# QKV of a transformer block on one core: normalized tokens turned by VectorE and moved within SBUF instead of turned by TensorE

## The chip, the core and the metric

The kernel runs on one core of a Trainium2 chip. TensorE (PE in the profile) multiplies, VectorE (DVE) and ScalarE (ACT) work on elements, GpSimd (POOL) does little here, and SyncE (SP) issues nearly every transfer. The metric is the device time of one execution in microseconds (us).

## The reference

One block of a diffusion transformer on 4096 tokens of 576 channels (2 batches of 2048), in float32, with 16 heads of 36 channels. Six vectors per batch come from a condition and shift, scale and gate the two halves.

```python
ada = silu(c) @ W_ada + b_ada
shift_msa, scale_msa, gate_msa, shift_mlp, scale_mlp, gate_mlp = split(ada, 6)
h = layernorm(x) * (1 + scale_msa) + shift_msa
x = x + gate_msa * attention(h, W_qkv, b_qkv, W_proj, b_proj)
h = layernorm(x) * (1 + scale_mlp) + shift_mlp
x = x + gate_mlp * (gelu(h @ W_fc1 + b_fc1) @ W_fc2 + b_fc2)
```

The change touches only the making of `h` for the first product, `h @ W_qkv`.

## The kernel before

The kernel has four phases: QKV (`phase_qkv`, the first 405 us of the span), attention, projection, MLP. Each engine has its own function (`sync`, `tensor`, `vector`, `scalar`, `gpsimd`), its instructions run in the order in which that function writes them, and semaphores join them.

QKV goes over the tokens in 8 chunks `c` of 512. A chunk has 13 steps `k`: four V steps (`k` 0 to 3, two products of 128 tokens by 288 channels each) and nine QK steps (`k` 4 to 12, called QK0 to QK8 here; one product of 128 channels by 512 tokens). Each product is 14 matmuls, since float32 accuracy is made of a high part (`hh`) and a rest (`lo`) of the tokens and of the weights. The product needs the tokens turned: channels on partitions. For that, the next chunk is prepared in ten pieces `n`, spread over the steps of the current one by the function `step(c, k)`, which all engines share:

- `n` 0 and 1: VectorE takes mean and variance of the token rows in `xin` (L823, L827), ScalarE the root (L953), VectorE the reciprocal;
- `n` 2 and 3: VectorE writes the normalized tokens into `xn` (L834), with 64 of the channels a second time, since the last of the five channel groups has only 64 and is held twice;
- `n` 5 to 9, one per channel group `kt`: TensorE turns four blocks of 128 by 128 into PSUM (`pt`, L667), ScalarE scales and shifts them into `hf` (L966), VectorE casts to `hh` (L846) and subtracts for `lo` (L849, L852).

`hf` has two buffers. From the second chunk on, `step` puts piece `n` at step `k = n`, so the last piece comes at `k` 9, which is QK5. A product of a chunk (L720) waits until all five `lo` of its own chunk are there (`s_lo`).

A QK result goes from PSUM (four buffers `pm`, shared with V) through ScalarE twice: `tf` (L1000) and its rounding `th` (L1001). VectorE subtracts for `tl` (L927), and SyncE stores `th` and `tl` to HBM (L628, L630). `tf`, `th` and `tl` have two buffers each, so ScalarE's L1000 of QKn waits until the stores of the QK two before have landed (`s_qo`). At QK2, SyncE loads `xin` for the chunk after next (L535), at V3 it stores V (L638). In the first chunks a row of the modulation (`modulation`, L682 on TensorE) lies in some QK steps; the step numbers are those of `mod_step`: one such product each in the chunks 0, 1, 2 and 3.

Of the kernel before, what the change touches and what calls it, by code (L numbers as in the profile page):

```python
# [7 lines left out]
F = mybir.dt.float32  # L8
# [7 lines left out]
C = 576  # L16
# [390 lines left out]
def phase_qkv(nc, A, ident, adaT, eps, bq, sc, qs0, ks0, qb0, hh0, lo0, mx, gd, xf, cond, W_ada,  # L407
# [46 lines left out]
    s_cond, s_ident, s_cz = A.sem("cond"), A.sem("ident"), A.sem("cz")  # L454
    s_ct, s_sc, s_am0, s_row0 = A.sem("ct"), A.sem("sc"), A.sem("am0"), A.sem("row0")
    s_vhi, s_vlo, s_qhi, s_qlo = A.sem("vhi"), A.sem("vlo"), A.sem("qhi"), A.sem("qlo")
    s_q0, s_q1, s_s, s_mx = A.sem("q0"), A.sem("q1"), A.sem("s"), A.sem("mx")
    s_nm, s_mt, s_mh, s_m = A.sem("nm"), A.sem("mt"), A.sem("mh"), A.sem("m")
    s_bv, s_bn, s_st, s_sd, s_rs, s_xn = (A.sem("bv"), A.sem("bn"), A.sem("st"), A.sem("sd"), A.sem("rs"),
                                          A.sem("xn"))  # L460
    s_tp, s_hf, s_hh, s_lo = A.sem("tp"), A.sem("hf"), A.sem("hh"), A.sem("lo")
    s_mm, s_tf, s_tl, s_vc, s_on = A.sem("mm"), A.sem("tf"), A.sem("tl"), A.sem("vc"), A.sem("on")
    s_qo, s_vo = A.sems("qo", 2), A.sems("vo", 2)

# [63 lines left out]

    def sync(e):
        def load(c):
            if c > 1:
                e.wait_ge(s_xn, c - 1)
            e.dma_start(xin[c % 2][:, :, :], xf[c * CH:(c + 1) * CH, :].rearrange("(t p) c -> p t c", p=128)).then_inc(  # L535
                s_x[c % 2], 16)
# [61 lines left out]
        def second_loads():  # L598
            e.wait_ge(s_mm, UN * (NCH - 1))
            e.wait_ge(s_q0, 128)  # L600
            for dst, r, src, f0, n, t, w in rows_b(qb0, ks0[:, LK:L], qkh, qkl, 0, C, 0):
                e.dma_start(dst[r:r + n, :].bitcast(F), src[f0:f0 + n, t:t + w]).then_inc(s_q1, 16)

        def max_rows():
            for j, m in enumerate((mh, ml)):
# [5 lines left out]
        for c in range(NCH):  # L611
            if c == HCH:
                first_loads()
            elif c == NCH - 1:
                second_loads()
            for kind, n in steps(c):
                if kind == "qk":
                    vi, p = mod_step(c, n)
                    if vi is not None:
                        modulation(vi, p)  # L620
                    if (c, n) == (NCH - 1, 7):
                        max_rows()
                    ft, j = c * NF + n, n % 2
                    if last(c, kind, n):
                        continue
                    rows, cols = slice(n * 128, n * 128 + 128), slice(c * CH, (c + 1) * CH)
                    e.wait_ge(s_tf, ft + 1)
                    e.dma_start(qkh[rows, cols], th[j][:, :].bitcast(F)).then_inc(s_qo[j], 16)  # L628
                    e.wait_ge(s_tl, ft + 1)
                    e.dma_start(qkl[rows, cols], tl[j][:, :].bitcast(F)).then_inc(s_qo[j], 16)  # L630
                    if n == 2 and c + 2 < NCH:
                        load(c + 2)
                elif n == 3:
                    b, k = divmod(c, HCH)
                    e.wait_ge(s_vc, 8 * (c + 1))
                    if c < 2:
                        e.wait_ge(s_on, c + 1)
                    e.dma_start(vd[b * H:(b + 1) * H, :, k * 4 * VW:(k + 1) * 4 * VW].rearrange("h p n -> p h n"),  # L638
                                vx[c % 2][:, :, :, :].rearrange("p h t d -> p h (t d)")).then_inc(s_vo[c % 2], 16)
        e.wait_ge(s_qo[0], 32 * (NCH * 5 - 1))  # L640
        e.wait_ge(s_qo[1], 32 * NCH * 4)
        for i in range(2):
            e.wait_ge(s_x[i], 16 * HCH)
            e.wait_ge(s_vo[i], 16 * HCH)
        for i in range(KT):
            e.wait_ge(s_wv[i], 16 if i < 4 else 32)
# [3 lines left out]
        e.wait_ge(s_wa, 128)  # L650
        e.wait_ge(s_bad, 128)
        e.wait_ge(s_gd, 32)
        e.wait_ge(s_q0, 128)
        e.wait_ge(s_q1, 128)
        e.wait_ge(s_m, 64)

    def tensor(e):
# [129 lines left out]
        for c in range(NCH):  # L787
            h, l = hh[c % 2], lo[c % 2]
            for k, (kind, n) in enumerate(steps(c)):
                if kind == "qk":  # L790
                    vi, p = mod_step(c, n)
                    if vi is not None:
                        modulation(vi, p)
                for m in maxima(c, kind, n):
                    score_max(m)
                if (c, kind, n) == (NCH - 1, "qk", 5):
                    max_rows()
                if (c, kind, n) == (0, "v", 0):
                    first_products()
                elif (c, kind, n) == (0, "v", 1):  # L800
                    pass
                elif kind == "qk":
                    product(c, 8 + n, passes(wh, wl, wm, wr, h, l, slice(n * 128, n * 128 + 128), slice(0, CH)),
                            pm[(c * UN + 8 + n) % 4][:, :])
                else:
                    for n2 in range(2):
                        u = 2 * n + n2
                        product(c, u, passes_t(wh, wl, wm, wr, h, l, slice(2 * C + n2 * HALF, 2 * C + (n2 + 1) * HALF),
                                               slice(n * 128, n * 128 + 128)), pm[(c * UN + u) % 4][:, 0:HALF])
                if c + 1 < NCH:  # L810
                    for p in step(c, k):
                        prepare(c + 1, p)

    def vector(e):
        def prepare(c, n):
            i = c % 2
            if n < 2:
                e.wait_ge(s_x[i], 16 * (c // 2 + 1))
                if c:
                    e.wait_ge(s_tp, KT * c)  # L820
                for t in range(2 * n, 2 * n + 2):
                    for g in range(2):
                        e.bn_stats(st[:, t, g, :], xin[i][:, t, g * HALF:(g + 1) * HALF]).then_inc(s_bn, 1)  # L823
            if n == 1:
                for t in range(4):
                    e.wait_ge(s_bn, 8 * c + 2 * t + 2)
                    e.bn_aggr(mv[:, t, :], st[:, t, :, :]).then_inc(s_st, 1)  # L827
                e.wait_ge(s_sd, c + 1)
                e.reciprocal(rs[:, :], sd[:, :]).then_inc(s_rs, 1)
            elif n in (2, 3):  # L830
                e.wait_ge(s_rs, c + 1)
                for t in range(2 * n - 4, 2 * n - 2):
                    for a, z, d in ((0, C, 0), (512, C, C)):
                        ins = e.tensor_scalar(xn[:, t, d:d + z - a], xin[i][:, t, a:z], mv[:, t, 0:1], rs[:, t:t + 1],  # L834
                                              ALU.subtract, ALU.mult)
# [112 lines left out]
    def scalar(e):  # L948
        def prepare(c, n):
            if n == 1:  # L950
                e.wait_ge(s_st, 4 * (c + 1))
                e.wait_ge(s_cz, 2)
                e.activation(sd[:, :], mv[:, :, 1], ACT.Sqrt, bias=eps[:, 0:1]).then_inc(s_sd, 1)  # L953
            elif 5 <= n < 10:
                kt, b = n - 5, c // HCH
                k = c * KT + kt
                j = k % 2
                e.wait_ge(s_tp, k + 1)
                if k > 1:
                    e.wait_ge(s_lo, k - 1)  # L960
                if k == 0:
                    e.wait_ge(s_row0, 9)
                if k < 3:
                    e.activation(hh[0][:, kt, :], pt[j][:, :], ACT.Identity, bias=adaT[:, 0, kt, b:b + 1],
                                 scale=adaT[:, 1, kt, b:b + 1]).then_inc(s_hh, 1)
                e.activation(hf[j][:, :], pt[j][:, :], ACT.Identity, bias=adaT[:, 0, kt, b:b + 1],  # L966
                             scale=adaT[:, 1, kt, b:b + 1]).then_inc(s_hf, 1)

        e.wait_ge(s_ct, 1)
# [1289 lines left out]
```

## Time and profile before

| | us |
|---|---|
| median of 3 runs (3258.19 to 3258.70) | 3258.28 |
| the profiled execution | 3255.73 |
| its span | 3254.0 |
| PE busy | 3238.2 (100%) |
| DVE busy | 2161.4 (66%) |
| ACT busy | 1695.6 (52%) |
| POOL busy | 358.3 (11%) |
| transfers on SyncE's queue, packets | 187582 (34.1% of 16 engines' span) |

The granted TensorE clock is 0.999 of full speed as a mean over the span. A busy TensorE says only that a matmul was in flight: matmuls overlap, so the pace is read from the distance of their starts, and a wait from the gap between an end and the next start.

### The profile page before, as it was taken

How to read it: one execution, taken by the hardware profiler on the slowest of the kernel's cores; microseconds unless marked ns; L12 is line 12 of the kernel's file. 1: busy time of each engine (PE TensorE's matmuls, PEld its weight loads, DVE VectorE, ACT ScalarE, POOL GpSimd, SP SyncE). 2: the span in 40 equal slices, each digit the busy share in tenths (PEclk: the TensorE clock that was granted, in tenths of full speed). 3: DMA queues.
4: the chain of work that ended last, by engine and by line, in shares of the span. 5: the costliest groups of instructions: out<-in, count | busy, mean ns of one | idle time of the engine just before them, and what ended most of it. 6: DMA issues, size and time to landing. Idle time of an engine off the chain costs nothing. (4 is left out here: it accounts for less than half of the span.)

```text
span 3254.0 us, 52481 instructions
## 1 busy us (share of the span) xinstructions
PE 3238.2 (100%) x19049; PEld 2117.3 (65%) x19049; DVE 2161.4 (66%) x4134; ACT 1695.6 (52%) x3183; POOL 358.3 (11%) x284
## 2 busy tenths in 40 slices
PE   9999999999999999999999999999999999999999
PEld 7888744444444444444444444449998898989988
DVE  6444488888888888888888888857633433433332
ACT  4323377777777777777777777765611112211110
POOL 0000010111100000010000000026411010000000
PEclk9999999999999999999999999999999999999999
DMA  7554442333323232323232333328722122421211
GB/s 241 179 165 149 153 93 59 75 74 76 66 59 66 59 65 56 68 63 69 59 69 59 65 63 65 63 63 276 238 95 77 53 82 71 142 69 57 80 46 55
DMA packets 187841, 299.53 MB, mean 92 GB/s; under 512 B 66783, under 2 KB 87791, under 8 KB 180670
## 3 DMA queue, kind: packets, MB, share of 16 engines
q1 hardware_dynamic: 187582, 296.17, 34.1%
q8 instruction: 151, 2.47, 0.3%
q14 instruction: 108, 0.88, 0.1%
HBM read 193.99 MB, written 101.43 MB: 91 GB/s over the span
## 5 line engine op out<-in xcount | busy, mean ns | idle before, releaser
L1306 DVE TENSOR_REDUCE q_mx<-b_st 128x1 f32<-128x512 f32 x1512 | 988.6, 681 | 147.8 <-PE b_st L1240 142.8
L1380 ACT ACTIVATE b_pt<-b_st 128x512 f32<-128x512 f32 x2048 | 1055.1, 609 | 8.6 <-PE b_st L1256 8.5
L1268 PE MATMUL b_op<-b_pt,b_vs 128*37 128x512 f32 x4096 | 981.5, 600 | 2.1 <-DVE b_ob L1349 2.1
L1373 ACT ACTIVATE b_early<-b_st 128x512 f32<-128x512 f32 x504 | 302.3, 600 | 451.3 <-PE b_st L1240 451.3
L1268 PEld LDWEIGHTS b_op<-b_pt,b_vs 128*37 128x37 f32 x4096 | 203.5, 113 | 444.3 <-issue 360.2
L2125 PE MATMUL d_pm<-d_vh,d_ah 128*128 128x288 f32 x1152 | 339.3, 295 | 0.8 <-DVE d_al L2163 0.8
L2126 PE MATMUL d_pm<-d_vl,d_ah 128*128 128x288 f32 x1152 | 339.5, 295 | 0.0
L2127 PE MATMUL d_pm<-d_vh,d_al 128*128 128x288 f32 x1152 | 339.5, 295 | 0.0
L1306 DVE TENSOR_REDUCE q_mx<-b_early 128x1 f32<-128x512 f32 x504 | 339.4, 673 | 0.0
L1444 POOL TENSOR_TENSOR w_oc<-b_oa,b_ob 37x512 f32<-37x512 f32 x127 | 161.3, 1270 | 1440.4 <-DVE b_ob L1349 1437.4
L1240 PEld LDWEIGHTS b_st<-q_hh,b_qa 36*128 36x128 f32 x1024 | 128.7, 184 | 223.5 <-DVE q_mx L1306 197.7
L1240 PEld LDWEIGHTS b_st<-q_ks,q_qs 36*128 36x128 f32 x992 | 125.1, 184 | 221.8 <-DVE q_mx L1306 193.6
L1240 PE MATMUL b_st<-q_hh,b_qa 36*128 36x512 f32 x1024 | 231.1, 444 | 0.0
L1240 PE MATMUL b_st<-q_ks,q_qs 36*128 36x512 f32 x992 | 225.8, 447 | 3.1 <-PEq L1025 2.0
L2174 DVE TENSOR_TENSOR d_ug<-d_pm,d_gt 128x288 f32<-128x288 f32 x128 | 58.5, 457 | 245.8 <-PE d_pm L2127 245.8
L2125 PEld LDWEIGHTS d_pm<-d_vh,d_ah 128*128 128x128 f32 x1152 | 216.2, 188 | 1.7 <-issue 1.0
L2126 PEld LDWEIGHTS d_pm<-d_vl,d_ah 128*128 128x128 f32 x1152 | 216.1, 188 | 0.7
L2127 PEld LDWEIGHTS d_pm<-d_vh,d_al 128*128 128x128 f32 x1152 | 216.2, 188 | 0.0
L1256 PE MATMUL b_st<-q_lo,q_ks 46*128 46x512 f32 x1024 | 205.6, 395 | 0.0
L1253 PE MATMUL b_st<-b_qa,q_hh 64*128 64x512 f32 x1024 | 205.5, 396 | 0.0
L1253 PE MATMUL b_st<-q_qs,q_ks 64*128 64x512 f32 x1024 | 205.3, 396 | 0.0
L1256 PE MATMUL b_st<-b_qb,q_hh 46*128 46x512 f32 x1024 | 204.9, 394 | 0.0
(414 smaller groups left out, 4685.7 us busy)
## 6 DMA issues: line engine op xcount, KB each, us to landing
qkh<-a_th SPq DMA_DIRECT2D x72, 256.0 KB, 2.1
qkl<-a_tl SPq DMA_DIRECT2D x72, 256.0 KB, 2.3
d_yi<-y SPq DMA_DIRECT2D x64, 288.0 KB, 3.0
n_oi<-hw SPq DMA_DIRECT2D x12, 1024.0 KB, 5.8
vd<-a_vx SPq DMA_DIRECT2D x8, 1184.0 KB, 6.6
b_vs<-vd SPq DMA_DIRECT2D x32, 296.0 KB, 3.0
a_x<-in_x SPq DMA_DIRECT2D x8, 1152.0 KB, 6.8
q_qs<-qkh SPq DMA_DIRECT2D x32, 288.0 KB
```

The lines of the kernel that those rows point to most:

```text
L1240: e.matmul(bank(slots[a])[:, :], qa[i][r, queries], ka[i][r, keys], start=True, stop=True).then_inc(s_s, 1)
L1253: e.matmul(bank(slots[a])[:, :], ka[i][r, keys], qa[i][r, queries], start=True, stop=False)
L1256: e.matmul(bank(slots[a])[:, :], kb[i][r, keys], qb[i][r, queries], start=False, stop=True).then_inc(s_st, 1)
L1268: ins = e.matmul(op[64 * a:64 * a + VW, :], vs[h % 2][:, j + 8 * a, :], pt[g % NP][:, a * 512:a * 512 + 512], start=j == 0, stop=j == 7)
L1306: e.tensor_reduce(mx[:, k // 2, col:col + 1], src, AX.X, ALU.max).then_inc(s_mx, 1)
L1373: e.activation(early[:, :], bank(slot)[:, :], ACT.Copy).then_inc(s_cp, 1)
L1380: e.activation(pt[g % NP][:, a * 512:a * 512 + 512], bank(k)[:, :], ACT.Exp, scale=SCALE).then_inc(s_p, 1)
L1444: e.tensor_tensor(oc[i][:, :], oa[i][:, :], ob[i][:, :], ALU.add).then_inc(s_oc, 1)
L2125: e.matmul(out, ah[:, f, ts], vh[:, f, cs], start=f == 0, stop=False)
L2126: e.matmul(out, ah[:, f, ts], vl[:, f, cs], start=False, stop=False)
L2127: ins = e.matmul(out, al[:, f, ts], vh[:, f, cs], start=False, stop=f == NT - 1)
L2174: e.tensor_tensor(ug[m % 2][:, :], pm[m % 4][:, 0:HALF], gt[:, b, cs], ALU.mult).then_inc(s_ug, 1)
```

## The change

Chunk 0 is prepared as before. For chunks 1 to 7, TensorE's four transposes per channel group are gone. Instead:

- a chunk of `xin` is loaded by four transfers of 32 partitions each, so that the tokens stand in the order that blocks of 32 by 32 need;
- VectorE no longer writes the 64 channels a second time; a new piece `n` 4 turns 32 by 32 blocks from `xn` back into `xin`, four instructions of 128 by 576;
- SyncE moves the turned blocks from `xin` into `xn`'s memory (`turned`) by 24 transfers of 32 partitions with runs of 512 bytes (`move`), written ahead of QK1's stores (QK3's in chunk 0);
- ScalarE reads `turned` in SBUF and waits for all 24 (`s_xl`);
- `step` has new places: pieces 5 to 9 come at `k` 9, 10, 10, 11, 12 (chunk 0: 10, 10, 11, 11, 12).

```diff
     def step(c, k):
         if c:
-            return range(k, k + 1)
-        return range(2) if k == 3 else range(k - 2, k - 1) if k in (4, 5) or 7 <= k < 12 else range(0)
+            return {9: range(5, 6), 10: range(6, 8), 11: range(8, 9), 12: range(9, 10)}.get(k, range(k, min(k + 1, 5)))
+        return {3: range(2), 4: range(2, 3), 5: range(3, 4), 6: range(4, 5), 10: range(5, 7), 11: range(7, 9),
+                12: range(9, 10)}.get(k, range(0))
...
+            for i in range(4):
+                rows = slice(c * CH + i * 128, c * CH + i * 128 + 128)
+                e.dma_start(xin[c % 2][i * 32:i * 32 + 32, :, :], xf[rows, :].rearrange("(t p) c -> p t c", p=32)).then_inc(
+                    s_x[c % 2], 16)
+
+        def move(c):
+
+            e.wait_ge(s_tp, KT + c)
+            blocks = xin[c % 2][:, :, :].rearrange("p t c -> p (t c)").rearrange("p (j r) -> p j r", r=128)
+            for i in range(4):
+                src, tok = blocks[i * 32:i * 32 + 32], slice(i * 128, i * 128 + 128)
+                for j in range(4):
+                    p, n = slice(j * 32, j * 32 + 32), 5 if j < 2 else 4
+                    e.dma_start(turned[p, 0:n, tok], src[:, j:4 * n - 3 + j:4, :]).then_inc(s_xl, 16)
+                    if j > 1:
+                        e.dma_start(turned[p, 4, tok], src[:, 14 + j, :]).then_inc(s_xl, 16)
...
                 if kind == "qk":
+                    if c + 1 < NCH and n == (1 if c else 3):
+                        move(c + 1)
...
-                if c + 1 < NCH:
-                    for p in step(c, k):
-                        prepare(c + 1, p)
...
+            elif n == 4 and c:
+                e.wait_ge(s_xn, c + 1)
+                blocks = xin[i][:, :, :].rearrange("p t c -> p (t c)").rearrange("p (j t c) -> p j t c", t=4, c=32)
+                for t in range(4):
+                    ins = e.transpose(blocks[:, :, t, :], xn[:, t, 0:C].rearrange("p (j c) -> p j c", c=32))
+                ins.then_inc(s_tp, 1)
...
-                e.wait_ge(s_tp, k + 1)
+                if c:
+                    e.wait_ge(s_xl, 16 * MOVES * c)
+                else:
+                    e.wait_ge(s_tp, k + 1)
...
-                e.activation(hf[j][:, :], pt[j][:, :], ACT.Identity, bias=adaT[:, 0, kt, b:b + 1],
+                e.activation(hf[j][:, :], turned[:, kt, :] if c else pt[j][:, :], ACT.Identity, bias=adaT[:, 0, kt, b:b + 1],
```

ScalarE at the end of chunk 1, from QK5 on, before (L1000 and L1001 write `tf` and `th`, L966 writes `hf`):

```order
L966 ACTIVATE a_hf<-a_pt,g_adaT 128x512 [waits a_s_lo,a_s_tp]
L1000 ACTIVATE a_tf<-a_pm,g_bq 128x512 [waits a_s_qo1,a_s_mm]
L1001 ACTIVATE a_th<-a_pm,g_bq 128x512
L966 ACTIVATE a_hf<-a_pt,g_adaT 128x512 [waits a_s_lo,a_s_tp]
L1000 ACTIVATE a_tf<-a_pm,g_bq 128x512 [waits a_s_qo0,a_s_mm]
L1001 ACTIVATE a_th<-a_pm,g_bq 128x512
L1000 ACTIVATE a_tf<-a_pm,g_bq 128x512 [waits a_s_qo1,a_s_mm]
L1001 ACTIVATE a_th<-a_pm,g_bq 128x512
L1000 ACTIVATE a_tf<-a_pm,g_bq 128x512 [waits a_s_qo0,a_s_mm]
L1001 ACTIVATE a_th<-a_pm,g_bq 128x512
```

And the same stretch of the changed kernel (L1032, L1033 and L998 are the same three lines):

```order
L998 ACTIVATE a_hf<-a_xn,g_adaT 128x512 [waits a_s_lo,a_s_xl]
L1032 ACTIVATE a_tf<-a_pm,g_bq 128x512 [waits a_s_qo0,a_s_mm]
L1033 ACTIVATE a_th<-a_pm,g_bq 128x512
L998 ACTIVATE a_hf<-a_xn,g_adaT 128x512 [waits a_s_lo,a_s_xl] x2
L1032 ACTIVATE a_tf<-a_pm,g_bq 128x512 [waits a_s_qo1,a_s_mm]
L1033 ACTIVATE a_th<-a_pm,g_bq 128x512
L998 ACTIVATE a_hf<-a_xn,g_adaT 128x512 [waits a_s_lo,a_s_xl]
L1032 ACTIVATE a_tf<-a_pm,g_bq 128x512 [waits a_s_qo0,a_s_mm]
L1033 ACTIVATE a_th<-a_pm,g_bq 128x512
L998 ACTIVATE a_hf<-a_xn,g_adaT 128x512 [waits a_s_lo,a_s_xl]
```

The last piece stood ahead of QK6's evacuation; now it stands behind QK8's, the last of the chunk.

SyncE in chunk 1, from QK0's second store to QK1's, in the changed kernel (L557 and L559 are the moves; before, QK1's store followed QK0's directly):

```order
L655 DMA qkl<-a_tl 128x512 [waits a_s_tl]
L557 DMA a_xn<-a_x 32x5x128 [waits a_s_tp]
L557 DMA a_xn<-a_x 32x5x128
L557 DMA a_xn<-a_x 32x4x128
L559 DMA a_xn<-a_x 32x128
L557 DMA a_xn<-a_x 32x4x128
L559 DMA a_xn<-a_x 32x128
```

These six stand there four times, and then QK1's stores, a modulation row, QK2's stores and the load of `xin` in four parts:

```order
L653 DMA qkh<-a_th 128x512 [waits a_s_tf]
L655 DMA qkl<-a_tl 128x512 [waits a_s_tl]
L585 DMA gd<-a_row 2x576 [waits a_s_row]
L653 DMA qkh<-a_th 128x512 [waits a_s_tf]
L655 DMA qkl<-a_tl 128x512 [waits a_s_tl]
L546 DMA a_x<-in_x 32x4x576 [waits a_s_xl]
L546 DMA a_x<-in_x 32x4x576 x3
```

On VectorE, the turning stands between QK0's `tl` and QK1's. TensorE's first V product of the next chunk, the consumer of all of it, still waits for the last `lo` and for a PSUM buffer:

```order
L744 MATMUL a_pm<-a_hh,a_wr 128x512
L744 MATMUL a_pm<-a_wh,q_hh 128x288 [waits a_s_tf,a_s_lo]
L744 MATMUL a_pm<-a_wl,q_hh 128x288
L744 MATMUL a_pm<-a_wh,q_lo 128x288
L744 MATMUL a_pm<-a_wh,q_hh 128x288
```

## Rows read from the trace of the kernel before

**Rows 1.** Waits from 60 to 350 us: who waited for whom, total, times, longest.

```profile
ACT a_tf L1000 <- PE a_pm L720: 128.9, 48, 8.1
...
ACT a_tf L1000 <- DMA qkl<-a_tl: 16.2, 5, 4.7
```

**Rows 2.** Stretches: us, busy PE, PEld, DVE, ACT, POOL, granted clock, DMA share, GB/s.

```profile
240.00:270.00 30.00, 30.00 (x164) 26.02 (x163) 13.51 (x25) 12.02 (x19) 0.00 (x0) 1.00 0.50 180
```

**Rows 3.** Timeline of TensorE in chunk 3: start, length, instruction.

```profile
204.28 0.60 PE L667 MATMUL a_pt<-g_ident,a_xn 128*128 128x128 f32 x4
...
207.92 0.39 PE L720 MATMUL a_pm<-a_hh,a_wh 128*128 128x512 f32 x1
...
210.87 0.39 PE L720 MATMUL a_pm<-a_hh,a_wr 128*128 128x512 f32 x1
211.19 2.69 PE L682 MATMUL a_sp<-a_wa,g_sc 128*2 128x288 f32 x20
```

**Rows 4.** Groups of instructions, first 600 us: count, busy us, mean ns, idle before.

```profile
L667 PE MATMUL a_pt<-g_ident,a_xn 128*128 128x128 f32 x160 | 23.8, 272 | 0.0
...
L834 DVE TENSOR_SCALAR a_xn<-a_x,a_mv,a_rs 128x576 f32<-128x576 f32 x64 | 24.1, 440 | 0.0
...
L1319 DVE STREAM_TRANSPOSE b_nt<-b_nm 128x32 f32<-128x32 f32 x14 | 3.0, 211 | 0.5
```

**Rows 5.** Timeline of TensorE: the last matmul of chunk 3.

```profile
216.89 0.39 PE L720 MATMUL a_pm<-a_hh,a_wr 128*128 128x512 f32 x1
```

**Rows 6.** Timeline of ScalarE in chunk 3.

```profile
190.43 0.78 ACT L966 ACTIVATE a_hf<-a_pt,g_adaT 128x512 f32<-128x512 f32 x1
...
196.53 0.68 ACT L1001 ACTIVATE a_th<-a_pm,g_bq 128x512 fp32r<-128x512 f32 x1
197.10 0.78 ACT L966 ACTIVATE a_hf<-a_pt,g_adaT 128x512 f32<-128x512 f32 x1
197.77 0.69 ACT L1000 ACTIVATE a_tf<-a_pm,g_bq 128x512 f32<-128x512 f32 x1
...
206.60 0.69 ACT L1000 ACTIVATE a_tf<-a_pm,g_bq 128x512 f32<-128x512 f32 x1 [3.84 <-DMA qkl<-a_tl]
...
217.32 0.69 ACT L1000 ACTIVATE a_tf<-a_pm,g_bq 128x512 f32<-128x512 f32 x1 [4.29 <-PE a_pm L720]
217.90 0.68 ACT L1001 ACTIVATE a_th<-a_pm,g_bq 128x512 fp32r<-128x512 f32 x1
```

**Rows 7.** Timeline of VectorE in chunk 3.

```profile
191.24 0.43 DVE L846 CAST q_hh<-a_hf 128x512 fp32r<-128x512 f32 x1
191.70 0.69 DVE L849 TENSOR_TENSOR q_lo<-a_hf,q_hh 128x512 fp32r<-128x512 f32 x1
...
218.62 0.69 DVE L927 TENSOR_TENSOR a_tl<-a_tf,a_th 128x512 fp32r<-128x512 f32 x1 [3.55 <-ACT a_th L1001]
```

**Rows 8.** Timeline of SyncE's issues: start, time of issuing, transfer.

```profile
25.23 1.11 SPq L481 DMA_DIRECT2D a_xn<-in_L_cond_W_qkv  x2
...
198.33 0.45 SPq L535 DMA_DIRECT2D a_x<-in_x  x1
...
199.79 0.32 SPq L630 DMA_DIRECT2D qkl<-a_tl  x1
...
221.79 0.37 SPq L596 DMA_DIRECT2D q_ks<-qkh  x1
...
224.26 0.39 SPq L596 DMA_DIRECT2D q_ks<-qkh  x1
```

**Rows 9.** Transfers from 60 to 350 us: count, KB each, median us from issue to landing.

```profile
qkl<-a_tl SPq DMA_DIRECT2D x55, 256.0 KB, 2.4
vd<-a_vx SPq DMA_DIRECT2D x6, 1184.0 KB, 6.4
```

**Rows 10.** Timeline of TensorE: first matmul behind the gap between QKV and attention.

```profile
407.44 0.50 PE L1240 MATMUL b_st<-q_ks,q_qs 36*128 36x512 f32 x2 [2.04 <-PEq L1025]
```

**Rows 11.** The stretch behind that gap, columns as in the second group.

```profile
409.00:414.50 5.50, 5.25 (x18) 2.96 (x19) 5.33 (x9) 4.73 (x10) 4.14 (x6) 0.50 0.95 264
```

More of the change, by code:

```diff
@@ L456, in phase_qkv @@
     s_vhi, s_vlo, s_qhi, s_qlo = A.sem("vhi"), A.sem("vlo"), A.sem("qhi"), A.sem("qlo")
-    s_q0, s_q1, s_s, s_mx = A.sem("q0"), A.sem("q1"), A.sem("s"), A.sem("mx")
+    s_q0, s_s, s_mx = A.sem("q0"), A.sem("s"), A.sem("mx")
     s_nm, s_mt, s_mh, s_m = A.sem("nm"), A.sem("mt"), A.sem("mh"), A.sem("m")
@@ L463, in phase_qkv @@
     s_qo, s_vo = A.sems("qo", 2), A.sems("vo", 2)
+    s_xl = A.sem("xl")
+    MOVES = 24
     vx0, vx1 = [q[:, :, :, :].rearrange("p h t d -> p (h t d)") for q in vx]
@@ L472, in phase_qkv @@
     sq = wa0[2:5] + [xf0[:, 0:2 * C], xf0[:, 2 * C:4 * C]]
+    turned = xf0.rearrange("p (k r) -> p k r", r=CH)
     V, QK = slice(2 * C, 3 * C), slice(0, 2 * C)
@@ L532, in load @@
         def load(c):
[L533 to L536, printed above, removed]
+            if c == 0:
+                e.dma_start(xin[0][:, :, :], xf[0:CH, :].rearrange("(t p) c -> p t c", p=128)).then_inc(s_x[0], 16)
+                return
+            if c == 2:
+                e.wait_ge(s_xn, 1)
+            elif c > 2:
+                e.wait_ge(s_xl, 16 * MOVES * (c - 2))
+            for i in range(4):
[12 more added lines that the diff above has]
+                        e.dma_start(turned[p, 4, tok], src[:, 14 + j, :]).then_inc(s_xl, 16)
         def columns(vi):
@@ L601, in second_loads @@
             for dst, r, src, f0, n, t, w in rows_b(qb0, ks0[:, LK:L], qkh, qkl, 0, C, 0):
-                e.dma_start(dst[r:r + n, :].bitcast(F), src[f0:f0 + n, t:t + w]).then_inc(s_q1, 16)
+                e.dma_start(dst[r:r + n, :].bitcast(F), src[f0:f0 + n, t:t + w]).then_inc(s_q0, 16)
         def max_rows():
@@ L642, in sync @@
         for i in range(2):
-            e.wait_ge(s_x[i], 16 * HCH)
+            e.wait_ge(s_x[i], 64 * HCH - 48 * (1 - i))
             e.wait_ge(s_vo[i], 16 * HCH)
@@ L652, in sync @@
         e.wait_ge(s_gd, 32)
-        e.wait_ge(s_q0, 128)
-        e.wait_ge(s_q1, 128)
+        e.wait_ge(s_q0, 256)
         e.wait_ge(s_m, 64)
@@ L817, in prepare @@
             if n < 2:
-                e.wait_ge(s_x[i], 16 * (c // 2 + 1))
-                if c:
-                    e.wait_ge(s_tp, KT * c)
+                e.wait_ge(s_x[i], 64 * (c // 2 + 1) - 48 * (1 - i))
+                if c == 1:
+                    e.wait_ge(s_tp, KT)
+                elif c:
+                    e.wait_ge(s_hf, KT * c)
                 for t in range(2 * n, 2 * n + 2):
@@ L832, in prepare @@
                 for t in range(2 * n - 4, 2 * n - 2):
-                    for a, z, d in ((0, C, 0), (512, C, C)):
+                    for a, z, d in ((0, C, 0),) if c else ((0, C, 0), (512, C, C)):
                         ins = e.tensor_scalar(xn[:, t, d:d + z - a], xin[i][:, t, a:z], mv[:, t, 0:1], rs[:, t:t + 1],
```

## The prediction, made before the changed kernel had run

> **What bounds the kernel now.** I read the stretches first: in QKV, TensorE is busy 30.00 of 30 us at full clock [rows 2]. Then the waits: from 60 to 350 us none is TensorE's; ScalarE waits 128.9 us for TensorE, and 16.2 us for the store that frees its buffers [rows 1]. So QKV runs at TensorE's pace. What TensorE no longer does is gained in full, and a wait of TensorE is lost in full, unless it is caught up, and an engine that is the bound has nothing to catch up with. The timelines then give the pace of each engine and the handovers, from which the new waits have to be worked out.
>
> **What is removed.** With one group of four transposes in it, a QK step takes from 204.28 to 207.92, 3.64 us. Without, 14 matmuls at a distance of (210.87 - 207.92)/13 = 0.227 us take 3.18 us [rows 3]. So a group of four costs 0.46 us, although the mean of one instruction is 272 ns [rows 4]: they overlap. There are 160 in all, 20 of them chunk 0's; 140 go, 35 groups by 0.46 = **-16.1 us**. The wait of transposes on `hf` goes too; it cost nothing. VectorE's 28 short second writes go, worth nothing either, since VectorE is busy 13.5 of 30 us [rows 2].
>
> **What the new order adds at each chunk's end.** Before, the last `hf` of the next chunk was made in step QK5, three steps (9.5 us) ahead of its use, and V followed QK8 without a gap: no wait of TensorE stands there [rows 1, 2]. Now ScalarE makes it behind QK8's evacuation, and the first V product waits for the `lo` made of it. Even with every engine ready, from the start of QK8's last matmul (216.89 in chunk 3 [rows 5]):
>
> - ScalarE begins `tf` at 217.32: 0.43; `th` 0.58 later [rows 6];
> - `hf` 0.57 after `th` (196.53 to 197.10), and it takes 0.78 [rows 6];
> - VectorE's `tl` begins at 218.62, 0.72 after `th`, and takes 0.69 [rows 7], which ends just when `hf` does; the cast begins 0.03 after `hf`'s end (190.43 + 0.78 = 191.21, then 191.24), the subtraction 0.46 after the cast, and takes 0.69 [rows 6, 7];
> - some 0.05 to TensorE, as in the other handovers.
>
> Sum 0.43 + 0.58 + 0.57 + 0.78 + 0.03 + 0.46 + 0.69 + 0.05 = 3.59, less the 0.23 at which the next matmul would have followed anyway [rows 3]: 3.36 us of wait. Nothing covers it: all PE work of the chunk is done, and the next chunk's needs this `lo`. Seven boundaries: +23.5 us, already more than the 16.1 saved. Piece by piece this is the surest term; its rows exist, only `hf`'s source is now SBUF.
>
> **What the moves add.** SyncE issues in order. The nearest rows of few partitions are the eight loads of 28 to 36 partitions: from 221.79 to 224.26 six distances, 0.41 us each [rows 8]. Bounds: 0.36 (a store's 0.32 [rows 8] and a gap of 0.04) and 0.56 (64 partitions, 1.11 for two [rows 8]) plus 0.04. I take 0.41, by 24 = 9.8 us (8.6 to 14.4). The data are 7 x 2560 packets of 512 bytes; a store of V, 2048 packets (16 by 128 rows of 592 bytes), lands in 6.4 us [rows 9], so the 2560 of a chunk need about 8.0 us with their latency, less than the issuing. VectorE's four turns of 128x576 have no row: a turn of 128x32 takes 211 ns, a pass over 576 columns 440 ns [rows 4], and a pass of 512 at 0.69 gives 0.78 for 576 [rows 7]. From 0.4 to 0.78; I take 0.70, 2.8 us, since the turn of 32 columns has no sign of the faster pass.
>
> The Trainium skill ("Vector Engine (DVE) Microarchitecture Reference", 3.8 The reshape front-end) says that the transpose sustains one element per cycle per lane. By that and the 0.96 GHz of "VectorE: DVE Perf Modes", 576 columns are an estimated 0.60 us, so 2.4 us for four; no row shows it, and the sum would be the same within 0.5 us a chunk.
>
> Now one chunk without a modulation product but with a load of `xin` (chunks 4, 5), in us from QK0's first matmul; QKn ends at 3.18(n+1) + 0.2:
>
> - `tf` of QK0 at 3.4, its `tl` done at 5.4, the turns at 8.2, the last move issued at 18.0;
> - QK1's stores stand behind the moves: `tl` issued at 18.4, landed 2.4 later [rows 9], 20.8. ScalarE can't begin QK3's `tf` before, where it began at 12.9. TensorE would need that buffer for QK7 at 22.3; `th` is ready at 22.1. So no stall there, by a hair;
> - QK2's stores, and the load of `xin` in four issues by 0.46, till 21.0. QK3's `tl` store is issued at 22.8 behind this load. In the row of such a store it was issued at 199.79, 1.46 after the load, and ScalarE went on at 206.60 [rows 6, 8], 8.2 after the load's issue. From the middle of the four issues that gives 28.2; I take 28 for QK5's `tf`;
> - from there ScalarE is the bound: `tf` and `th` 1.17 a pair, `hf` 0.67 each [rows 6]. QK6 29.8, two `hf`, QK7 32.4, one, QK8 34.2, and the last `hf` 35.4 to 36.1; 1.25 to the `lo` and TensorE: 37.4. V could have begun at 28.6: **8.8 us** of wait.
>
> Chunk 6 has no load: QK5's `tf` at 25.2, V at 34.6, 6.0. Chunks 1 to 3 have a modulation product of 2.6 to 2.7 us [rows 3] on TensorE, which puts off its own need: 8.8 - 2.7 = 6.1 each. Chunk 0 moves two steps later, with load ahead of moves, and has a modulation product too: tf of QK5 at 27.1, last `lo` at 37.2, need at 31.3: 5.9. Sum 2 x 8.8 + 6.0 + 3 x 6.1 + 5.9 = **+47.8 us**, the 23.5 of the order being part of it.
>
> **The clock.** A gap of 2.04 us at the end of QKV [rows 10] was followed by 5.5 us at a granted clock of 0.50, which is 1.2 in place of 2.4 GHz [rows 11]: 5.25 us busy at half pace, 2.6 lost. The seven new gaps are each longer. I take 2.6 for each, **+18.2 us**; bounds 0 (if the clock rides over such a gap) and, since each stretch may be longer than this one, 3.5.
>
> **The sum**: -16.1 + 47.8 + 18.2 = +49.9 on the profiled execution's 3255.7, 3305.6. The median of runs is 2.5 above that execution, which I keep: **3308 us**.
>
> **Rivals.**
> 1. The moves hide, only the order costs. If the stores behind them get through in time (shorter issues, a load that passes aside), each gap is 3.36: +23.5 - 16.1 = +7.4, 3266 without any drop of the clock, 3284 with it. For it: TensorE needs QK3's buffer only at 22.3, and ScalarE waits for TensorE 128.9 us in all [rows 1], which is room to catch up. Against it: 24 by even 0.36 still puts the last issue at 16.8. The Trainium skill ("DMA: Bandwidth & Descriptors", Issuing engines are not separate DMA queues) speaks for it: the time on the sequencer to start transfers is "usually small relative to the DMA itself". By that rule the moves would hold SyncE for little. The trace disagrees for transfers this small: 0.41 us of issue [rows 8] for one twenty-fourth of some 8 us, and nothing gained.
> 2. The moves are slower than issued: 0.60 us each, because the issues cost what those of 64 partitions do, or because all read from 32 partitions. The last move is then 4.6 us later, at 22.6, QK3's `tf` at 25.4, TensorE stands at QK7 for about 4.7, and all behind is later: about 4.6 x 7 = +32 more, 3340.
> 3. Faster: the gap at a boundary falls under 16.1/7 = 2.3 us, from where the removed transposes decide. For that the last `hf`, cast and subtraction would have to take 1.5 us in place of 2.5, with SBUF as source and no queue behind the moves. Full gain if the gap vanished, 3242; at a gap of 2.0, 3256. Against it: ScalarE's order alone holds `hf` back, and its rows vary by under 5%.
> 4. The change doesn't do what it says: should TensorE keep transposes or the moves be done earlier, no wait appears. The order shows the opposite.
>
> **How the numbers follow.** Forecast 0.62 (own range 3288 to 3330), rival 1 0.16, rival 2 0.16, rival 3 0.03, nothing to be told 0.03. Less than 0.2% (6.5 us) is no change that a measurement of this kernel tells. The range 3270 to 3344 leaves out rivals 3 and the lower part of 1 and upper part of 2. Faster 0.03, same 0.03, slower 0.94.
>
> **What would show it.** In the profile after: TensorE waits for VectorE's L881 seven times, 6 to 9 us each, over 40 us in sum, ahead of the first V product; granted clock 0.5 for some us behind each; L691 counts 20. ScalarE's waits for DMA `qkl` rise from 16 to 60 us or more. Move issues 0.41 us apart. QK steps end at 3.18 us. Wrong would be the forecast if gaps are 3.4 us (rival 1), if TensorE stands in the middle of a chunk (rival 2), or if no drop of the clock follows a gap of 6 us.

## The result and the profile after

| | before | after |
|---|---|---|
| median of 4 runs, us | 3258.24 (3257.81 to 3258.70) | 3363.82 (3361.08 to 3369.03) |
| profiled execution's span, us | 3254.0 | 3367.3 |
| TensorE's first matmul of attention, us | 407.44 | 515.24 |
| TensorE busy, us | 3238.2 | 3253.8 |

The changed kernel is slower: ratio 1.0324, 95% interval 1.0311 to 1.0337, 105.6 us where 50 were forecast. The direction was right, and the three costs of the forecast (order, moves, slower clock) are there; the size was not: 3363.8 lies above the range, and TensorE also stands in mid-chunk, where the forecast had no wait. The first matmul of attention moved by 107.8 us [rows 10], so nearly all of the loss is in QKV; the rest of the span differs by 5.5 us, and by 1 to 5.5 in the other versions.

The waits of the changed kernel from 20 to 520 us; before, TensorE had none in the middle of QKV and ScalarE waited 16.2 us for stores [rows 1]:

```profile
ACT a_tf L1032 <- DMA qkl<-a_tl: 150.1, 20, 18.1
...
PEld a_pm L744 <- DVE a_hh L881: 34.6, 4, 14.3
PE a_pm L744 <- DVE a_hh L881: 32.7, 3, 13.9
PE a_pm L744 <- ACT a_th L1033: 31.7, 6, 6.6
PEld a_pm L744 <- DVE q_hh L881: 28.2, 3, 11.1
PE a_pm L744 <- DVE q_hh L881: 26.9, 3, 10.6
...
PE a_sp L727 <- ACT a_hf L998: 3.1, 1, 3.1
```

The PE rows are the loss. TensorE waits at two places of a chunk: for the last `lo` of the next one (L881), 59.6 us at six boundaries and 3.1 at the seventh (behind a score product there), and in six of seven chunks for ScalarE's evacuation (L1033), 31.7 us. Sum 94.4. The PEld rows are the weight loads ahead of the same matmuls, not to be added. ScalarE's row says why: 150.1 us of waits for stores.

SyncE's issues in chunk 1, from QK0's second store on (start, time of issuing):

```profile
104.91 0.32 SPq L655 DMA_DIRECT2D qkl<-a_tl  x1
107.58 1.93 SPq L557 DMA_DIRECT2D a_xn<-a_x  x3
109.55 0.60 SPq L559 DMA_DIRECT2D a_xn<-a_x  x1
...
123.34 0.60 SPq L559 DMA_DIRECT2D a_xn<-a_x  x1
123.98 0.58 SPq L653 DMA_DIRECT2D qkh<-a_th  x1
124.61 0.43 SPq L655 DMA_DIRECT2D qkl<-a_tl  x1
...
126.36 2.05 SPq L546 DMA_DIRECT2D a_x<-in_x  x4
```

A move holds SyncE for 0.60 us, 0.65 from start to start, where 0.41 was read off [rows 8]. The block of 24 takes 16.4 us, from 107.58 to 123.98 (15.9 to 16.5 in the other chunks), and only then QK1's stores go. On ScalarE it looks so, in the same chunk; the bracket is its idle time before, and what ended it:

```profile
109.24 0.69 ACT L1032 ACTIVATE a_tf<-a_pm,g_bq 128x512 f32<-128x512 f32 x1 [1.91 <-PE a_pm L744]
...
127.06 0.69 ACT L1032 ACTIVATE a_tf<-a_pm,g_bq 128x512 f32<-128x512 f32 x1 [16.56 <-DMA qkl<-a_tl]
```

And on TensorE, at QK7 of chunk 1 and at the boundary behind it:

```profile
128.47 0.77 PE L744 MATMUL a_pm<-a_hh,a_wh 128*128 128x512 f32 x1 [3.73 <-ACT a_th L1033]
...
147.03 0.61 PE L744 MATMUL a_pm<-a_wh,q_hh 128*128 128x288 f32 x1 [10.63 <-DVE q_hh L881]
```

The clock behind that boundary (columns as in [rows 2]): 0.60 as a mean over six us, part of them at half clock, then full:

```profile
147.00:153.00 6.00, 5.97 (x29) 5.97 (x30) 0.46 (x1) 0.00 (x0) 0.00 (x0) 0.60 0.87 275
153.00:160.00 7.00, 7.00 (x55) 7.00 (x55) 5.06 (x17) 0.30 (x1) 0.00 (x0) 1.00 0.02 4
```

Of VectorE and TensorE in the changed kernel, by groups, as in [rows 4]:

```profile
L691 PE MATMUL a_pt<-g_ident,a_xn 128*128 128x128 f32 x20 | 2.9, 275 | 0.0
...
L865 DVE STREAM_TRANSPOSE a_x<-a_xn 128x576 f32<-128x576 f32 x28 | 19.2, 744 | 0.0
L857 DVE TENSOR_SCALAR a_xn<-a_x,a_mv,a_rs 128x576 f32<-128x576 f32 x32 | 17.2, 574 | 0.0
```

20 transposes are left, as forecast, and a turn takes 744 ns where 0.70 was taken.

To make an account, I took QKV in stretches of 1 us and summed TensorE's idle time, and its busy time by (1 - granted clock) as what the slower clock lost. For the changed kernel 94.4 idle and 28.4 of clock, from 34 us to the last matmul of QKV; with the 16.1 us saved, 94.4 + 28.4 - 16.1 = 106.7, against 107.8 measured at attention's first matmul. For the kernel before both are zero. The same account, over the same part, is given for each version below; for E1 (which saves nothing) to E9 it meets the shift of attention's first matmul within 1.1 us.

### The profile page after: what moved, and what is told of

Its sections match the earlier page's. It is cut to its first block and busy times, and to the rows that moved or that the text cites. A ratio compares the mean times of both kernels' runs of the same rounds, so it can differ in the third digit from the quotient of the medians.

```text
span 3367.3 us, 52354 instructions
## 1 busy us (share of the span) xinstructions
PE 3253.8 (97%) x18909; PEld 2131.1 (63%) x18909; DVE 2172.8 (65%) x4134; ACT 1694.6 (50%) x3183; POOL 358.7 (11%) x284
```

## The experiments

All are timed against the kernel before on the same chip. Its medians were 3256.9 (E1 to E4), 3258.5 (E5 to E8) and 3260.2 us (E9 to E11), so the ratios compare versions of different groups better than the medians. E5 is not in the table: it was executed once, for its issues (3338.6 us).

| version | median us | ratio (95%) | idle | clock |
|---|---|---|---|---|
| changed kernel | 3363.8 | 1.0324 (1.0311 to 1.0337) | 94.4 | 28.4 |
| E1 order only | 3286.4 | 1.0089 (1.0074 to 1.0104) | 20.9 | 8.3 |
| E2 no moves | 3277.9 | 1.0064 (1.0049 to 1.0079) | 22.0 | 12.4 |
| E3 24 small moves | 3361.3 | 1.0318 (1.0303 to 1.0334) | 91.2 | 26.5 |
| E4 4 wide moves | 3290.8 | 1.0101 (1.0085 to 1.0118) | 33.3 | 16.8 |
| E6 last piece earlier | 3358.3 | 1.0308 (1.0294 to 1.0322) | 86.7 | 29.5 |
| E7 moves spread | 3338.2 | 1.0245 (1.0231 to 1.0259) | 81.2 | 14.7 |
| E8 rebuilt, 16 moves | 3251.7 | 0.9978 (0.9968 to 0.9988) | 4.4 | 1.7 |
| E9 15 of 24 moves | 3324.6 | 1.0200 (1.0186 to 1.0214) | 62.3 | 18.2 |
| E10 rebuilt, even lots | 3248.4 | 0.9964 (0.9952 to 0.9977) | 1.3 | 0.0 |
| E11 rebuilt, half on GpSimd | 3250.7 | 0.9970 (0.9959 to 0.9981) | 3.3 | 0.0 |

**E1: the order alone.** The kernel before, with only `step` replaced:

```diff
 # before.py
-            return range(k, k + 1)
-        return range(2) if k == 3 else range(k - 2, k - 1) if k in (4, 5) or 7 <= k < 12 else range(0)
+            return {9: range(5, 6), 10: range(6, 8), 11: range(8, 9), 12: range(9, 10)}.get(k, range(k, min(k + 1, 5)))
+        return {3: range(2), 4: range(2, 3), 5: range(3, 4), 6: range(4, 5), 10: range(5, 7), 11: range(7, 9),
+                12: range(9, 10)}.get(k, range(0))
```

> The kernel before, with only the places of the pieces 5 to 9 of the change (last channel group at QK8); TensorE still turns. My theory: ScalarE makes the last hf behind QK8's evacuation, so TensorE waits at each of 7 boundaries 3.4 us less the 0.5 us that its own transposes take: +20 us, and up to 18 more if the clock falls behind each gap: 3278 to 3297. Rival A (the order costs nothing, all of the loss is the moves): 3258. Rival B (the order is most of the loss of 106 us): above 3320.

Measured 3286.4, 29.5 above before. TensorE's gap is 2.77 or 2.78 us at six boundaries, as here, and 1.68 ahead of a score product at the seventh:

```profile
73.26 0.40 PE L721 MATMUL a_pm<-a_wh,a_hh 128*128 128x288 f32 x1 [2.78 <-DVE a_hh L853]
...
221.26 0.63 PE L668 MATMUL a_pt<-g_ident,a_xn 128*128 128x128 f32 x4 [2.26 <-ACT a_hf L967]
```

2.78 us where 3.4 - 0.5 = 2.9 was expected; the second row is another wait, for a free `pt` ahead of the last transposes, in one chunk. The order costs by itself, and rival A falls; so does rival B, since this is far from the whole loss.

**E2: no moves.**

```diff
-                e.wait_ge(s_xl, 16 * MOVES * (c - 2))
+                e.wait_ge(s_tp, KT + c - 2)
...
         def move(c):
             e.wait_ge(s_tp, KT + c)
-            for i in range(4):
-                ...
-                    e.dma_start(turned[p, 0:n, tok], src[:, j:4 * n - 3 + j:4, :]).then_inc(s_xl, 16)
+            return
...
-                    e.wait_ge(s_xl, 16 * MOVES * c)
+                    e.wait_ge(s_tp, KT + c)
```

> The changed kernel without the 24 transfers of move() (what ScalarE reads is then not the turned tokens). VectorE's turns, the four loads and the places stay. My theory: 3258 - 16 + 23.5 = 3266, to 3284 if the clock falls behind each gap. Rival B (order and turns are most of the loss): above 3320.

Measured 3277.9, inside of what was expected; rival B falls. The gaps, the first two of seven:

```profile
70.94 0.40 PE L738 MATMUL a_pm<-a_wh,a_hh 128*128 128x288 f32 x1 [3.25 <-DVE a_hh L875]
120.71 0.61 PE L738 MATMUL a_pm<-a_wh,q_hh 128*128 128x288 f32 x1 [3.24 <-DVE q_hh L875]
```

3.24 us against 3.36 forecast: five of the six boundaries have 3.24 or 3.25, one 3.31, and the gap ahead of the score product at the seventh is 2.15. The clock differs behind gaps of the same length: behind the first it stayed at full, 1.00 from 70 to 78 us, and the next matmul took 0.40; behind the second it was 0.57 as a mean from 120 to 124 us, and the matmul took 0.61. This version has the turns, the four loads and the order, and costs 20.9 us; the changed kernel's other 84.7 us (105.6 less 20.9, each against its own before) are the moves.

**E3 and E4: issues or bytes.** E3 keeps 24 transfers but cuts each to one run; E4 keeps the bytes and packets but in 4 transfers of 128 partitions.

```diff
 # E3
-                    e.dma_start(turned[p, 0:n, tok], src[:, j:4 * n - 3 + j:4, :]).then_inc(s_xl, 16)
+                    e.dma_start(turned[p, 0, tok], src[:, j, :]).then_inc(s_xl, 16)
 # E4
+                e.dma_start(turned[:, 0:5, i * 128:i * 128 + 128], blocks[:, i:13 + i:3, :]).then_inc(s_xl, 16)
```

> The changed kernel with all 24 transfers a chunk, but each moves only one run of 512 bytes a partition (16 KB), 384 KB a chunk in place of 1310 KB. Theory of the issue (each transfer holds SyncE 0.65 us, whatever it carries): 3355 to 3364, as the changed kernel. Rival C (the bytes moved within SBUF hold up the stores behind them): nearer to the kernel without moves, under 3310.

> The changed kernel with the same 1310 KB and 2560 packets a chunk, but in 4 transfers of 128 partitions in place of 24 of 32 partitions (what lands is not the turned tokens). Theory of the issue: 20 issues by 0.65 = 13 us fewer ahead of QK1's stores, so near the kernel without moves: 3268 to 3292. Rival C (bytes): 3350 to 3364.

Measured 3361.3 and 3290.8. Over the version without moves, 24 issues with 29% of the bytes cost 83.4 us, 4 issues with all bytes 13.0, both together 84.7. So nearly all of the cost is in the number of issues; rival C falls as the main cause. SyncE in E3, and then in E4:

```profile
171.77 1.80 SPq L557 DMA_DIRECT2D a_xn<-a_x  x3
173.61 0.59 SPq L559 DMA_DIRECT2D a_xn<-a_x  x1
...
187.66 0.58 SPq L653 DMA_DIRECT2D qkh<-a_th  x1
```

```profile
152.14 3.16 SPq L554 DMA_DIRECT2D a_xn<-a_x  x4
155.35 1.09 SPq L648 DMA_DIRECT2D qkh<-a_th  x1
156.48 0.96 SPq L650 DMA_DIRECT2D qkl<-a_tl  x1
```

An issue of 16 KB holds SyncE for 0.59 us, one of 80 KB in the changed kernel for 0.61; the block is 15.9 us long, like there. In E4 a wide one (320 KB) takes 0.79 to 0.80 in five of the seven chunks, 1.2 to 1.3 in two, and the stores behind it 1.09 and 0.96, where they took 0.58 and 0.43 behind the changed kernel's moves: there the bytes do show.

**E5: what makes an issue dear.** 20 transfers a chunk, whose form changes by chunk:

```diff
+                n = (128, 64, 48, 36, 28, 32, 36)[c - 1]
+                src = blocks[0:n, i % 18, :] if c < 6 else xf[c * CH + i:c * CH + i + n, 0:128]
+                e.dma_start(turned[0:n, kt, tok], src).then_inc(s_xl, 16)
```

> A look at the issuing time alone: the changed kernel with 20 transfers a chunk of one run of 512 bytes a partition, whose number of partitions differs by chunk: 128, 64, 48, 36, 28 within SBUF, then 32 and 36 from HBM (what lands is not the turned tokens). Theory D (few partitions make an issue dear): the time rises from 0.36 us at 128 to 0.65 at 64 and below. Theory E (source and target both in SBUF make it dear): 0.65 for all five within SBUF, about 0.4 for the two from HBM. Theory F (the number divided over the 16 queues): 0.65 where the number is a multiple of 16 other than 128 (64, 48, 32), 0.4 at 36 and 28, which divide over 12 and 14.

The issues of its one execution (start, time of all 20):

```profile
53.03 13.18 SPq L557 DMA_DIRECT2D a_xn<-a_x  x20
103.96 13.79 SPq L557 DMA_DIRECT2D a_xn<-a_x  x20
165.51 13.34 SPq L557 DMA_DIRECT2D a_xn<-a_x  x20
226.22 15.80 SPq L557 DMA_DIRECT2D a_xn<-a_x  x20
290.15 15.92 SPq L557 DMA_DIRECT2D a_xn<-a_x  x20
352.46 10.36 SPq L557 DMA_DIRECT2D a_xn<-in_x  x20
409.88 9.54 SPq L557 DMA_DIRECT2D a_xn<-in_x  x20
```

Within SBUF 0.66, 0.69, 0.67 us each for 128, 64 and 48 partitions, 0.79 and 0.80 for 36 and 28; from HBM 0.52 for 32 and 0.48 for 36. Theories D and F fall: 128 partitions are as dear, and 36 and 28 dearer still. E is the nearest: source and target both in SBUF make the issue dear. The cleanest pair is 36 partitions, 0.79 within SBUF and 0.48 from HBM. Each form stands in one chunk only, but the place in QKV is not what differs: in the changed kernel, whose moves all have one form, a move took 0.66 to 0.69 in every chunk. The account is not full: 20 in a row from HBM are also above the 0.41 of eight in a row [rows 8], and why 36 and 28 partitions are dearer stays open. That row was what the prediction read its price from, and it is of another kind.

**E6: the last piece a step earlier**, in the changed kernel.

```diff
-            return {9: range(5, 6), 10: range(6, 8), 11: range(8, 9), 12: range(9, 10)}.get(k, range(k, min(k + 1, 5)))
-        return {3: range(2), 4: range(2, 3), 5: range(3, 4), 6: range(4, 5), 10: range(5, 7), 11: range(7, 9),
-                12: range(9, 10)}.get(k, range(0))
+            return {9: range(5, 6), 10: range(6, 8), 11: range(8, 10)}.get(k, range(k, min(k + 1, 5)))
+        return {3: range(2), 4: range(2, 3), 5: range(3, 4), 6: range(4, 5), 10: range(5, 7), 11: range(7, 10)}.get(k, range(0))
```

> The changed kernel with only the last piece one step earlier (ahead of QK8's evacuation on ScalarE), moves as they are. With the moves in place ScalarE is late anyway and works through a backlog, so the order is worth one evacuation, 1.2 us, and no more than 2 a boundary: 8 to 14 us less than the changed kernel, 3350 to 3356. Rival (each boundary gains the full 3.4 us of the order and its clock): 3322 or less.

Measured 3358.3, 5.5 below the changed kernel where 8 to 14 were expected, and not clear of noise (by ratios, 1.0308 against 1.0324, the intervals overlap). In the traces TensorE idles 86.7 us against 94.4, 1.1 a boundary, which is the one evacuation that was expected; the clock loses 1.1 more. The rival falls: with the moves in place the order hardly counts, and its 3.24 a boundary (E2) must not be added to what the moves cost. The prediction had not added them either.

**E7: the moves spread** in lots of five behind the stores of QK0 to QK4.

```diff
+                    if c + 1 < NCH:
+                        g = n - (0 if c else 2)
+                        if 0 <= g < 5:
+                            moves(c + 1, 5 * g, min(5 * g + 5, 24))
```

> The changed kernel with the 24 transfers no longer in one block ahead of QK1's stores but in lots of five behind the stores of QK0 to QK4 (QK2 to QK6 in chunk 0). If the harm is that the stores stand behind the block, the waits at QK7 vanish and the ones at the boundary shrink: 3310 to 3335. Rival (it is SyncE's total time, 15.6 us of issues and then the last piece, that counts, wherever they stand): 3345 to 3365, the waits at QK7 gone but those at the boundary longer.

Measured 3338.2, between the two expectations. The waits at QK7 are gone, and those at the boundary are longer (17.0 us ahead of chunk 1, 10.0 to 12.5 later, 8.8 ahead of the score product), 81.2 in sum against 94.4:

```profile
85.02 0.61 PE L752 MATMUL a_pm<-a_wh,a_hh 128*128 128x288 f32 x1 [16.99 <-DVE a_hh L889]
...
320.35 0.61 PE L752 MATMUL a_pm<-a_wh,a_hh 128*128 128x288 f32 x1 [12.53 <-DVE a_hh L889]
```

So both theories hold in part: the blocked stores cost the waits in mid-chunk, and the wait for the last piece stays. That this rest is the length of 24 issues, which start behind QK0 wherever they stand, is argued from the rival, not shown by a run of its own. Half of the gain is clock: seven gaps in place of 13 lose 14.7 us in place of 28.4.

**E8: rebuilt.** The 64 last channels are turned twice by VectorE, with `xin` 640 wide, so 16 transfers do for 24; statistics, normalizing and turns are done in the V steps; lots of four transfers; `xin` is loaded later; the last piece stands at QK7, ahead of QK8's evacuation; chunk 1 stays with TensorE. It changes all of these at a time.

```diff
-            return {9: range(5, 6), 10: range(6, 8), 11: range(8, 9), 12: range(9, 10)}.get(k, range(k, min(k + 1, 5)))
+            return {0: (0, 1), 1: (2,), 2: (3, 4), 3: (10,), 9: (5, 6), 10: (7, 8), 11: (9,)}.get(k, ())
...
+            for j in range(4):
+                e.dma_start(turned[j * 32:j * 32 + 32, :, i * 128:i * 128 + 128], src[:, j:17 + j:4, :]).then_inc(s_xl, 16)
...
-                    if n == 2 and c + 2 < NCH:
+                    if n == (5 if c else 2) and c + 2 < NCH:
                         load(c + 2)
```

> The same idea rebuilt by what was found: 16 transfers in place of 24 (the last 64 channels are turned twice by VectorE instead of being moved twice), the turns done in the V steps, the transfers in lots of four ahead of QK0's stores and behind those of QK0, QK1, QK2, the load of the tokens behind QK5's stores, the last piece at QK7, and chunk 1 still turned by TensorE. My theory: no wait of TensorE is left, 30 groups of transposes by 0.46 us are saved: 3258 - 13.8 = 3244. Rival: a lot of four, 2.6 us, and two stores fill a step of 3.2 us, ScalarE comes late at QK6 or later, and gaps of some us come back with a slower clock behind them: 3258 to 3290.

Measured 3251.7, ratio 0.9978: 0.2% faster than the kernel before, half of what was expected. Four boundaries still have a gap, the longest here:

```profile
257.26 0.40 PE L741 MATMUL a_pm<-a_wh,a_hh 128*128 128x288 f32 x1 [1.91 <-DVE a_hh L882]
```

The half that is missing is in the trace: of the 13.8 us saved, 4.4 are lost idle, 1.7 to the slower clock and 0.8 by a longer gap ahead of attention (2.84 for 2.04), which leaves 6.9, against 6.1 by which attention starts earlier.

**E9: my own block length.** 15 of the 24 transfers.

```diff
-    MOVES = 24
+    MOVES = 15
...
-                    e.dma_start(turned[p, 0:n, tok], src[:, j:4 * n - 3 + j:4, :]).then_inc(s_xl, 16)
-                    if j > 1:
-                        e.dma_start(turned[p, 4, tok], src[:, 14 + j, :]).then_inc(s_xl, 16)
+                    m += 1
+                    if m < 16:
+                        e.dma_start(turned[p, 0:n, tok], src[:, j:4 * n - 3 + j:4, :]).then_inc(s_xl, 16)
```

> The changed kernel with 15 of the 24 transfers of a chunk (the eight of the doubled channels and one more are left out, so part of what ScalarE reads is not the turned tokens). 15 by the measured 0.65 us are 9.8 us, just the length that the prediction gave the block of 24. If only the length of an issue was mis-sized there, this runs at the predicted time, 3300 to 3316. If another step of the walk from store to last piece is off too, it is outside of that.

Measured 3324.6, outside: more than the length of an issue was off. Chunk 4 began its QK0 3.4 us ahead of its first evacuation at 270.63, at 267.2. Its SyncE, then its ScalarE:

```profile
275.31 10.80 SPq L560 DMA_DIRECT2D a_xn<-a_x  x15
286.16 0.59 SPq L654 DMA_DIRECT2D qkh<-a_th  x1
286.79 0.45 SPq L656 DMA_DIRECT2D qkl<-a_tl  x1
...
288.28 2.28 SPq L546 DMA_DIRECT2D a_x<-in_x  x4
...
291.27 0.34 SPq L656 DMA_DIRECT2D qkl<-a_tl  x1
```

```profile
289.26 0.69 ACT L1033 ACTIVATE a_tf<-a_pm,g_bq 128x512 f32<-128x512 f32 x1 [11.02 <-DMA qkl<-a_tl]
...
298.19 0.69 ACT L1033 ACTIVATE a_tf<-a_pm,g_bq 128x512 f32<-128x512 f32 x1 [5.92 <-DMA qkl<-a_tl]
```

From QK0's start: turns done at 8.1 (forecast 8.2), the block 10.8 long in place of 9.8 (9.6 to 10.8 over the chunks, 10.3 on average), QK3's `tf` at 22.1 (20.8), QK5's `tf` at 31.0 (28.0). The store behind the load of `xin` went at 291.27 and ScalarE at 298.19, 9.9 us after the load's first issue, where the prediction had 8.9 (8.2, read off a load of one transfer, counted from the middle of the four issues). So the mis-sized issue was the larger error, and not the only one.

**E10 and E11: two more steps on E8.** Lots of 4, 3, 3, 3, 3; and half of the transfers on GpSimd.

```diff
 # E10
-                    if 0 < c < NCH - 1 and n < 3:
-                        move(c + 1, n + 1)
+                    if 0 < c < NCH - 1 and n < 4:
+                        moves(c + 1, 4 + 3 * n, 7 + 3 * n)
 # E11, in gpsimd
+        for c in range(2, NCH):
+            e.wait_ge(s_tp, 2 * KT + c - 1)
+            for i in (2, 3):
+                ...
+                for j in range(4):
+                    e.dma_start(turned[j * 32:j * 32 + 32, :, i * 128:i * 128 + 128], src[:, j:17 + j:4, :]).then_inc(s_xp, 16)
```

> The rebuilt version with its 16 transfers in lots of 4, 3, 3, 3, 3 (ahead of QK0's stores and behind those of QK0 to QK3) in place of 4, 4, 4, 4. If the remaining waits of TensorE (0.5 to 1.9 us at four boundaries) come from stores that a lot of four holds up, they go: 3246 to 3250. Rival: the last transfer comes later, QK5's piece waits for it, and the time stays at 3250 to 3254.

> The rebuilt version with half of its 16 transfers issued by GpSimd, which is idle in QKV, and half by SyncE. If issuing on one queue is what binds, SyncE has 5 us less and the waits at the boundaries go: 3244 to 3249. Rival: GpSimd issues so much slower, over 1.3 us each, that the last piece comes late, 3255 or more.

E10 measured 3248.4, ratio 0.9964, the fastest version here, though its interval overlaps E8's; that even lots help is seen in the trace, where the waits fall from four to one. Its TensorE waits from 60 to 400 us (the first is the gap ahead of attention, 2.04 before [rows 10]):

```profile
PE b_st L1274 <- PEq L1059: 3.0, 1, 3.0
PE a_pm L742 <- DVE a_hh L883: 1.1, 1, 1.1
```

One gap of 1.1 us is left, and attention starts at 396.42, 11.0 us earlier than before. E11 measured 3250.7, no better than E8 by their intervals, and missed both what was expected and its rival. GpSimd issued its eight in 4.5 to 4.7 us, faster than SyncE, but SyncE's four beside them took 4.7 to 6.5 us, 5.4 in four of the six chunks, where the same lot takes 3.9 to 4.3 in E8 and E10. The slowest:

```profile
229.40 6.47 SPq L555 DMA_DIRECT2D a_xn<-a_x  x4
```

```profile
229.66 4.53 POOL L1064 DMA_DIRECT2D a_xn<-a_x  x8 [44.48 <-DVE a_x L866]
```

So an issue's time isn't SyncE's alone: SyncE issues slower beside GpSimd. Whether GpSimd is slowed too no run shows, and what they share stays open. Nor is the time fixed on SyncE alone. In each chunk of E8 and E10 the first lot of four, some 1.5 us behind V's store of 1184 KB, takes 3.9 to 4.3 us, a later one mostly 0.64 a transfer, as in E10:

```profile
86.84 3.96 SPq L555 DMA_DIRECT2D a_xn<-a_x  x4
...
91.96 1.90 SPq L555 DMA_DIRECT2D a_xn<-a_x  x3
```

Whether V's store is the cause was not tried.

## Why the prediction was right in direction and wrong in size

**What is removed, -16.1 us: right.** E1 and E2 have the same order, one with TensorE's transposes, one without. Attention begins at 437.78 and at 425.85, -11.9 us; E2 has 1.1 more idle and 4.1 more of the clock, which leaves -17.1 for the 35 groups.

**The order, 3.36 us a boundary: right**, 3.24 to 3.31 measured at six boundaries of E2 (2.15 of the seventh shows, behind the score product). It is a pure chain of durations, and each had a row but the 0.05 of the last handover.

**The turns: right, in part by luck**, 0.74 for 0.70. The lower bound of 0.4 rested on the 440 ns of [rows 4], which is a mean over two forms; 128x576 alone took 573 ns in the kernel before.

**The moves: the step that failed.** The prediction took "six distances, 0.41 us each" from loads of HBM into SBUF, with a top of 0.60, for transfers within SBUF, which the kernel before has none of. They take 0.65, and the block 15.9 to 16.5 us in place of 9.8. Sorted by number of partitions, the row looked like the nearest; the memory in which source and target lie was the property that counted (E5), and there it was the farthest. With the longer block the prediction's "no stall there, by a hair" at QK7 fails too: 31.7 us of waits stand there. Rival 2 had the dearer issue and its sign, TensorE standing at QK7: 4.7 us forecast, 3.0 to 6.6 measured. Its reasons, the few partitions, were not the right ones (E5), it got 0.16, and its price, 32 us over the forecast, was too small: it counted no slower clock behind the gaps at QK7. Rival 1, that the moves hide, falls: without them the time is 3277.9.

**The walk behind the block: a second size.** Near the block's forecast length (E9, 10.3 on average for 9.8) TensorE idles 62.3 us where 47.8 were forecast. Per chunk 7.9, 9.3, 8.7, 8.3, 11.4, 10.9, and 5.7 plus what is hidden behind the score product, where 5.9, 6.1, 6.1, 6.1, 8.8, 8.8 and 6.0 were forecast: 2 to 3 us each for the first six. In chunk 4, QK5's `tf` was 3.0 late: 1.0 came from the block, 0.3 from the first stores and 1.7 from the store behind the split load. In the prediction I had read this last number off a load that one transfer made.

**The clock: right in kind, the number of gaps wrong.** 28.4 us were lost in 13 gaps, 2.2 each, where 2.6 were taken for seven. E9's seven gaps of 5 to 10 us lost 18.2, 2.6 each; its three of 0.7 to 1.0 us lost nothing. E2's seven, six of 3.2 to 3.3 us and one of 2.15, lost 12.4, 1.8 each, and behind equal gaps the clock sometimes fell and sometimes not.

In sum: forecast -16.1 + 47.8 + 18.2 = 49.9; measured -16.1 + 94.4 + 28.4 = 106.7. Of the 46.6 us more of idle time, 14.5 are there already with E9's 15 issues, most of it the walk, and 32.1 come with the longer block. The 10.2 us more of clock come with the six gaps at QK7. The range was too narrow since its errors go the same way, and since I took 0.60 as the top without a transfer of that kind to look at.

## What to carry to other kernels

Here a transfer cost its issuing queue 0.6 us whether it carried 16 or 80 KB, and 0.79 or more with 320 KB: count the issues ahead of the store that someone waits for, and price them with a row that has the same source and target memory, or with wide bounds if there is none. Before work is taken off the bound engine, check that the last instruction of what replaces it stands ahead of the previous stage's last evacuation, since a handover chain at a stage's end is paid at every stage (E1), unless a longer wait covers it (E6). A wait that is cut out of the middle of a stage also gives back the slower clock behind it (E7). The same idea went from 3% slower to 0.4% faster by fewer issues, an earlier start, an earlier last piece and even lots, with the arithmetic unchanged; what each of the first three gave was not taken apart.

## What the runs showed of the hardware that I had not expected

- Issuing on SyncE: a store from SBUF to HBM 0.32 us by itself and 0.58 right behind the moves, 20 in a row of 512-byte runs from HBM into SBUF 0.48 to 0.52 each, 20 within SBUF 0.66 to 0.69, and 0.79 to 0.80 for 36 and 28 partitions, at 14 to 64 KB each.
- Of gaps of 3.24 and 3.25 us in one run (E2), one left the clock at full, the others were followed by half clock. Of E1's six gaps of 2.8 us four were followed by half clock, two not; 8.3 us in all were lost. A gap of 1.91 us in E8 was followed by half clock as well.
- VectorE's `tensor_scalar` of 128x576 took 574 ns in the changed kernel [rows 4: 440 before]. The mean in the group before held the 64-column instructions as well (128x64, 308 ns; 128x576 alone 573), so nothing had become slower; the row was a mean over two forms.
